# Three edits to a 16-image fused kernel: two attention blocks in flight, samples turned in spare bank columns, four block numbers read by one load

## The reference, cut to what matters

```
_, idx = jax.lax.top_k(logits, TOPK)                    # TOPK = 4 of 49
kv_sel = jax.vmap(lambda t, i: t[i])(kv_pix, idx)
att = jnp.einsum('bpqhd,bpkhd->bphqk', q_pix * SCALE, k_sel)   # 64 x 256, 4 heads
att = jax.nn.softmax(att, axis=-1)
o = jnp.einsum('bphqk,bpkhd->bpqhd', att, v_sel)
xh = xh + (o + lepe) @ wo_w + wo_b                      # lepe: 5x5 depthwise conv
xh = xh + gelu(ln(xh) @ mlp_w1 + mlp_b1) @ mlp_w2 + mlp_b2
```

```
om = conv3x3(offset_feat, w_offmask) + b_offmask        # 216 channels
val = bilinear samples of feat_up at (y + ky + dy, x + kx + dx), times mask
out = relu(einsum('bgckhw,ogck->bohw', val, wr) + b_dcn) + x
```

## Time and profile before

| | |
|---|---|
| median of three runs | 13883.27 us |
| profiled execution | 13886.23 us |
| its span | 13883.2 us (3.0 us lie around it) |
| busy: PE, PEld | 10537.0 (76%), 8028.7 (58%) |
| busy: DVE, ACT, POOL | 8448.6 (61%), 8917.4 (64%), 6916.6 (50%) |
| mean granted TensorE clock | 0.918 of full |

### The profile page before, as it was taken

One profiled execution on the slowest core, in us unless ns is written; L12 is line 12 of the kernel. 1 busy time (PEld: TensorE's weight loads), 2 busy tenths in 40 slices (PEclk: granted clock), 3 DMA queues, 4 the chain that ended last, 5 costly groups with the idle time before them and its releaser, 6 DMA issues.

```text
span 13883.2 us, 501225 instructions
## 1 busy us (share of the span) xinstructions
PE 10537.0 (76%) x187900; PEld 8028.7 (58%) x187900; DVE 8448.6 (61%) x11589; ACT 8917.4 (64%) x18708; POOL 6916.6 (50%) x6167
## 2 busy tenths in 40 slices
PE   3567887878787787878778787877878787741787
PEld 2346665666666666666666666666666666631666
DVE  6446667575666657576666757666675766631743
ACT  1246666667666676766666676666667666741677
POOL 0024554545455454545445454544545454566467
PEclk7679999999999999999999999999999999976999
DMA  4134444445444444444444444444444444431444
GB/s 127 47 78 112 117 113 114 114 109 122 109 117 113 115 116 109 122 110 118 113 116 115 109 121 110 118 111 118 115 109 119 112 118 111 120 75 29 107 128 115
DMA packets 1847066, 1517.08 MB, mean 109 GB/s; under 512 B 1006688, under 2 KB 1381984, under 8 KB 1841568
## 3 DMA queue, kind: packets, MB, share of 16 engines
q1 hardware_dynamic: 1834468, 1474.31, 42.7%
q0 software_dynamic: 9216, 2.38, 0.2%
HBM read 1297.68 MB, written 178.25 MB: 106 GB/s over the span
## 4 chain that ended last, share of the span: by engine, by line
PE 29%; issue 18%; DVEq 12%; ACT 9%; DVE 9%; POOLq 8%; SPq 6%; POOL 6%; DMA 2%; ACTq 1%
PE bank_small L952 6%; DVEq L1478 6%; PE bank_scores L871 5%; PE bank_small L1003 5%; POOLq L658 4%; PE windows L982 4%; DVEq L1463 4%; DVE ol L1479 3%; POOLq L660 3%; POOL gbuf L729 2%; ACT hats L1193 2%; SPq L496 2%; PE bank_post L925 2%; ACT hats L1197 1%; SPq L493 1%
## 5 line engine op out<-in xcount | busy, mean ns | idle before, releaser
L1533 DVE TENSOR_TENSOR prod<-windows,wy 128x640 f32<-128x640 f32 x4032 | 3283.7, 818 | 2036.0 <-PE windows L982 1933.9
L982 PEld LDWEIGHTS windows<-fx,hats 64*64 64x64 f32 x129024 | 2661.1, 139 | 1363.0 <-issue 1292.5
L982 PE MATMUL windows<-fx,hats 64*64 64x80 f32 x129024 | 3293.8, 243 | 181.9 <-issue 148.2
L657 POOL TENSOR_TENSOR prod<-prod 128x768 f32<-128x768 f32 x1344 | 2487.0, 1850 | 1364.8 <-DVE prod L1533 1357.3
L1193 ACT ACTIVATE hats<-hats,cst 128x512 f32<-128x512 f32 x4032 | 2879.1, 714 | 166.6 <-DMA hats<-sample_columns 96.8
L1479 DVE SCALAR_TENSOR_TENSOR ol<-xpad,lepw,ol 128x448 f32<-128x448 f32 x2688 | 2442.1, 909 | 240.9 <-issue 8.0
L1197 ACT ACTIVATE hats<-hats 128x512 f32<-128x512 f32 x4032 | 2517.2, 624 | 6.8
L871 PE MATMUL bank_scores<-ksel,qbd 128*128 128x256 f32 x3136 | 963.7, 434 | 1035.4 <-DVE ob L1464 893.2
L659 POOL TENSOR_TENSOR prod<-prod 128x384 f32<-128x384 f32 x1344 | 1563.0, 1163 | 214.9 <-issue 26.8
L662 POOL TENSOR_TENSOR val<-prod 128x384 f32<-128x384 f32 x1344 | 1497.7, 1114 | 241.1 <-issue 156.2
L952 PE MATMUL bank_small<-wom,ofp 128*128 128x216 f32 x8064 | 1609.4, 355 | 0.0
(11 more groups left out here) (193 smaller groups left out, 13333.4 us busy)
## 6 DMA issues: line engine op xcount, KB each, us to landing
hats<-sample_columns SPq DMA_DIRECT2D x2688, 336.0 KB
ksel<-k_windows SPq DMA_DIRECT2D x3136, 32.0 KB
vsel<-v_windows SPq DMA_DIRECT2D x3136, 32.0 KB
fx<-map_columns SPq DMA_DIRECT2D x64, 420.0 KB
xpad<-in_x SPq DMA_DIRECT2D x17, 1568.0 KB, 13.3
q_windows<-qb SPq DMA_DIRECT2D x112, 224.0 KB, 2.6
k_windows<-kb SPq DMA_DIRECT2D x112, 224.0 KB, 3.5
v_windows<-vb SPq DMA_DIRECT2D x112, 224.0 KB, 3.2
```

Source lines behind the costliest of these rows:

```text
L657: pool.tensor_tensor(v[:, :, 0:n], v[:, :, 0:n], v[:, :, n:2 * n], ALU.add)
L982: last[h] = pe.matmul(o[m], hat[:, m], fx[XP * h:XP * h + XP, g, row:row + WR, :].rearrange("p r c -> p (r c)"), start=True, stop=True)
L1533: dve.tensor_tensor(o, x, w.unsqueeze(3).to_broadcast([128, 2, CP * WR, CG]), ALU.mult).then_inc(s_wm, 1)
```

## The change

**Attention.** A second bank, `bank_scores2`, takes every other block (`bank_of(w)`). A block's steps are spread over six slots where they took three: scores in its slot 0, maxima and exponentials in slot 1, turning in slot 2, copying in slot 3, value products in slot 4, scaling in slot 5. A block still begins every three slots. The scores of block w wait for the scaling of block w-2. On DVE the scaling now stands ahead of the maxima and of the taps of its slot. `P0` and what follows from it (post, pooling, gate) move two slots later.

**Samples.** The bank `bank_turned` is gone. The nine transposes of a tile are done in five pairs (the fifth has one) in columns 320 to 447 of the two banks of `hb`, right behind the windows of that slot, in slots 14 to 18 after the tile's start instead of 13, 14 and 16. DVE copies them (five copies of 128x256, the last 128x128) where ACT did three of 128x384. DVE waits for the transposes ahead of `weigh`, and copies behind it. PE's windows two slots later wait for that copy. `valt` has two buffers. `deform` and the relu move from slot 8 of the next tile to slot 5 of the tile after it, `finish` and the store one tile later. The turned columns go to columns 344 to 471 of `bank_small`, and the sum of what lies outside follows one slot later, as does the flag.

**SP.** One call loads the four numbers of a block, without a bounds check, and eight DMAs follow.

```diff
-OM, PXT, VT, WD, WYH = 0, 2, (4, 5, 7), 8, 2
+OM, PXT, WD, WYH = 0, 2, 5, 2
+VT, NP = Q + 5, 5
-P0 = A0 + BSL + 1
+P0 = A0 + BSL + 3
+SPARE = CP * WR * CG
+        def bank_of(w):
+            return (bs, bs2)[w % 2]
...
-                for m in range(TOPK):
-                    v = sp.value_load(sel[0:1, w * TOPK + m:w * TOPK + m + 1], min_val=0, max_val=P2 - 1)
+                _, chosen = nc.values_load_multi_w_load_instructions(
+                    sel[0:1, w * TOPK:(w + 1) * TOPK], engines=[mybir.EngineType.SP], min_val=0, max_val=P2 - 1,
+                    skip_runtime_bounds_check_because="they are places of maxima among P2 logits")
+                for m, v in enumerate(chosen):
...
-                wait(pe, s_os, cnt(i, P2, w))
+                else:
+                    wait(pe, s_os, cnt(i, P2, w - 1))
...
+            def turn_samples(i, t, p, bank):
+                pe.wait_ge(s_vok, cnt(i, NT, t + 1))
+                for k in range(2 * p, min(2 * p + 2, KK)):
+                    mm = pe.transpose(bank[:, k % 2, SPARE:SPARE + 128], val[t % 2][:, k * 128:(k + 1) * 128], ident)
+                mm.then_inc(s_vt, 1)
             def windows(i, t, q):
+                bi, bt = (i, t) if q >= 2 else before(i, t, 1)
+                if bi is not None:
+                    bi, bt, p = pair_of(bi, bt, (q - 2) % Q)
+                if bi is not None:
+                    pe.wait_ge(s_ve, cnt(bi, NP * NT, NP * bt + p + 1))
...
             def x_first(i, n):
-                m = n - A0
-                if 0 <= m < SWIN * P2 and m % SWIN == 0:
-                    scores(i, m // SWIN)
-                if 0 <= m < SWIN * P2 and m % SWIN == 2:
-                    pv(i, m // SWIN)
+                w = step_of(n, 4)
+                if w is not None:
+                    pv(i, w)
+                w = step_of(n, 0)
+                if w is not None:
+                    scores(i, w)
...
+            def copy_samples(i, t, p, bank):
+                dve.wait_ge(s_vt, cnt(i, NP * NT, NP * t + p + 1))
+                wait(dve, s_do, cnt(i, NT, t - 1))
+                k = min(2, KK - 2 * p)
+                dve.tensor_copy(valt[t % 2][:, 2 * p:2 * p + k, :], bank[:, 0:k, SPARE:SPARE + 128]).then_inc(s_ve, 1)
...
                         if di is not None:
+                            bi, bt, p = pair_of(di, t, q)
+                            if bi is not None:
+                                dve.wait_ge(s_vt, cnt(bi, NP * NT, NP * bt + p + 1))
                             weigh(di, t, q)
-                        if xi is not None and r == 0 and 0 <= w < P2:
-                            maxes(xi, w)
-                        if fi is not None and q == PXT + 1:
+                            if bi is not None:
+                                copy_samples(bi, bt, p, hb[n % 2])
+                        if xi is not None:
+                            w = step_of(n, 5)
+                            if w is not None:
+                                scale_heads(xi, w)
+                            w = step_of(n, 1)
+                            if w is not None:
+                                maxes(xi, w)
+                        if fi is not None and q == PXT + 2:
                             flags(fi, ft)
                         if xi is not None:
                             x_slot(xi, n)
-                            if r == 2 and 0 <= w < P2:
-                                scale_heads(xi, w)
```

## The result

| | before | changed | ratio, 95% interval |
|---|---|---|---|
| median, us | 13887.76 (7 runs in all, 4 beside the changed kernel) | 13683.06 (4 runs, 13678.01 to 13709.62) | 0.9855, 0.984 to 0.987 |
| profiled execution, us | 13886.23 | 13709.62 | |
| its span, us | 13883.2 | 13707.8 | |

A forecast was written before the change was run, and what follows sets the result against it. Attention was taken as where a pass spends its time, with PE and DVE near 75% and SP's queue as full. Gains of 345 + 165 + 45 + 20 + 80 = 655 us gave 13231 us, range 12850 to 13700.

The forecast's parts named there:

- Image 0: Attention alone, 49 blocks: two banks shorten the block ring; 80 us gained, bounds 30 and 147.
- the ring of 4.9: Image 0: with two banks the next scores follow the turning, 4.9 us a block instead of 7.8.
- The one load: SP's queue: one load saves 2.0 us a block, 7 us a pass at the start; condition for part 1.
- The rival that leaned on the page: SP's issue time bounds nothing, so only the start's 7 us a pass are lost: 13335 us, chance 0.05.
- the rival of the load that does nothing: SP stays as full; start's 7 us lost, stretch loses at most 10: 13530 us, chance 0.05.
- Elsewhere and the last pass: Other 104 slots: 3 us a pass, 45 us; last pass: 20 us, as most PE waits go.
- The stretch from 81 to 207: Attention with side work: 435 us falls to 412, 345 us over 15 passes.
- I leave 15 of the 64.5 us: Slots 81 to 207: of DVE's waits before maxima, products and offsets' bias, 15 us stay.
- part 1: Two blocks in flight: scores no longer stand behind the last scaling; 64.5 us of DVE's waits can go.
- My signs of being right: Attention stretch: PE's scores wait under 15 us, DVE's maxima wait near zero, blocks every 9.8 us; image 0's every 6 to 7.
- waits move: Exponentials stay tied to their slot's maxima; stretch falls 5 us, start 7, image 0 40: 13665 us, chance 0.12.
- The slower rival: DVE's copies cost more than the ring gives, 27 us a stretch on the path: 14086 us, chance 0.08.

The follow-up runs named there:

- short copies: VectorE's copies of the turned samples cut to 4 of every 128 columns, against the changed kernel: 13471.41 us, 0.9697 of the kernel before.
- the later sum outside: Sum of what lies outside taken one slot later on PE, against the changed kernel: differs by 11 us by the medians, intervals overlap.
- one bank: Attention put back to one bank and three slots a block, samples and one load kept, against the changed kernel: 13727.3 us, 0.9877 of the kernel before.
- maxima first: Maxima put ahead of the product in their slot on VectorE, against the changed kernel: 292 us less.
- short sums: GpSimd's row sums cut to one of 16 columns, against the changed kernel: 12923.69 us, 0.9298 of the kernel before.

## Why the prediction was right or wrong

**Image 0: right.** Forecast 80 us, measured 103, of them 97 by the second bank. Scores follow each other at 410.52 and 415.65 us where 7.8 us lay between them:

```profile
410.52 2.04 PE L901 MATMUL bank_scores<-ksel,qbd 128*128 128x256 f32 x4 [0.33 <-DMA vsel<-v_windows]
...
415.65 1.76 PE L901 MATMUL bank_scores<-ksel,qbd 128*128 128x256 f32 x4 [0.77 <-issue]
```

That is 5.1 us, near the ring of 4.9 that I took as the bound. Over all 49 blocks, with the bands of post between them, the maxima follow each other every 8.65 us before and every 6.39 us in the changed kernel: the 6 to 7 us of the forecast.

**The one load: right, and for more than I gave it.** 8.5 us a pass in slots 59 to 81 against the 7 of the sum; SP's waits in a stretch rose from 27 to 86 us. Between a values DMA and the next keys DMA lie 6868.83 - 6868.65 = 0.18 us where there were 0.79:

```profile
6868.18 0.47 SPq L526 DMA_DIRECT2D vsel<-v_windows  x1
6868.83 0.45 SPq L524 DMA_DIRECT2D ksel<-k_windows  x1
```

That the load is a condition for the rest was right in the sum, not in the place: within the change it is worth 245 us, of which 74 are in image 0 and 8.5 a pass in slots 59 to 81, but only 2.7 us a stretch. It decides even the sign: with the four loads the changed kernel is slower than the one before. The rival that leaned on the page did not come: the Trainium skill says ("DMA: Bandwidth & Descriptors", "Issuing engines are not separate DMA queues") that initiating a DMA usually takes the sequencer little time relative to the DMA itself. That sentence is about the initiation, and no run here tests it. What these runs removed is the register work between the issues. In the rival of the load that does nothing the sum does not fit its sentence: it takes 195 us, 13 a stretch, where it says 10.

**Elsewhere and the last pass: small errors.** The slots outside 59 to 207 sum to -1.9 us a pass against the 3 I took, as the sum of larger parts: +7.0 in slots 9 to 53, where short copies give back 4.3 of it and the later sum outside 2.0, and -7.1 in 207 to 225. In the last pass I read that DVE "hides the copies". It does not: its products wait 152.0 us for transposes, and the pass is 13 us longer instead of 20 shorter. The changed kernel and the eight others here that have the same last pass take 534 to 554 us for it, the three with the copies on ACT 522 to 525, the two without the samples part 520. The price that I set near zero, the added wait ahead of `weigh`, is 15.2 us in a stretch, inside my bounds of 0 and 42, and large where PE is the late one:

```profile
DVE prod L1571 <- PE windows L998: 152.0, 82, 4.6
```

**The stretch from 81 to 207: wrong.** The failing step is "I leave 15 of the 64.5 us", with the premise below it that part 1, by freeing PE from the scaling, would free DVE. Of the 64.5 us 28.3 are left, but 31.0 are left with one bank too: the second bank freed DVE of nearly nothing there, and added 10 us in post, which I had left as it was. My account of DVE was 313 busy + 16 own + 27 copies + 41 post + 15 = 412 us. The trace has 349 busy (313 + 27 + 9, mostly slower taps less the overlap), 17 own, 45 in post and 28 other, which is 439 us. So of the 27 us that were missing 13 are other waits, 9 DVE's busy time, 4 post and 1 its own. The term that the sum did not have at all is the slower taps and sum of the attention, 21 us by groups. The named wait of PE did go, and it was not what set the time: with one bank the stretch is 8 us shorter with that wait in place. My signs of being right misled in the same way. PE's wait before scores, DVE's before maxima, SP's waits and image 0's blocks all came as foreseen; the distance of blocks in the stretch, 10.5 us and not 9.8, was the one that told the time. The change spreads the steps over more slots, but keeps the maxima behind the product in the same slot as the exps, the exps ahead of the post step on ACT, and puts the scaling between. ACT then stands 84 us, the GELU comes late, and PE and DVE wait for it, with PE's products behind it at the lower clock. Turning these orders takes the stretch from 439.8 to 409.2 us, near the 412 of the forecast, by a mechanism that it did not contain. Of the rivals it was "waits move" whose condition held ("the exponentials stay tied to the maxima of their slot"); its stretch of -5 us was still too good. That its time, 13665 us, is near the measured one is luck: it has neither the 7.1 us a pass gained in slots 207 to 225 nor the 7.0 lost in 9 to 53, and it gives image 0 40 us where 103 came.

The slower rival had the right sign for the stretch, +5 us where it said up to +27. But the copies cost the path less than it said: taking them off DVE gives back 9 of the 27 us, as the taps beside POOL's sums then take longer. What it left out is that the ring gives something in image 0 and the load much at the start, and these decide the sign of the whole.

**What stays open.** How much of the 20 us a stretch of "maxima first" is the wait itself and how much the clock that follows it was not separated: every order that shortened the waits of the changed kernel also shortened its time at the lower clock. Nor was it tried why the place of the scaling weighs so much: at the end of the slot it costs 42 us a stretch, and ahead of the product, beside the maxima, it gives another 5. And why a tap takes longer when the copies are gone was not tried.

## What to carry to other kernels

When a wait of a neighbouring engine has a named cause, ask what the engine that everyone waits for would do sooner if it went; in the long stretch here the answer was nothing, and 50 us of PE's idle time were worth less than nothing, while in image 0 the same wait was the whole ring and its removal gave 97 us. Where several engines are tied in one slot, the place of a short step within the slot is a term of its own: put first what another engine needs in the same slot, and try that before any change of buffers. Count a copy that moves to another engine not only by its duration but by what it does to the queue that it joins: on ACT it gained 105 us in one order and lost 52 in another.

## What the runs showed of the hardware

**Taps against POOL's sums.** A tap, a DVE instruction with two inputs from SBUF, 128x448, takes 684 ns with POOL idle, and on average 694 with short sums, 920 before, 984 with one bank, 1030 in the changed kernel, and 1073 and 1089 there with the copies short or on ACT; why more of it falls beside the sums was not separated. The product, which reads one operand from a bank, stays at 816 to 819 ns in all of these. The Trainium skill has the rule ("SBUF — State Buffer", "Who interferes with whom"): a DVE instruction with two SBUF inputs contends with a GpSimd instruction that reads SBUF. The trace agrees. Of the 920 ns in the earlier trace rows a quarter was already the sums' doing.

**The clock within a busy stretch.** The granted clock fell to the lower level while PE stood 4.59 us with 0.30 us of work in 4 us, and six products took 4.85 us in place of 2.52. So the wait cost another 2.33 us behind it, and the same came behind all 60 waits of 3.7 to 4.7 us in that place, at 1.5 to 2.3 us each.
